# Mamba's rows of B and C put on all partitions by DMA, products with B on GpSimd, decays in PSUM

## What is computed

```python
def step(h, inp):
    d, b, c, ut = inp
    dA = jnp.exp(d[:, :, None] * A)
    h = dA * h + (d * ut)[:, :, None] * b[:, None, :]
    y = jnp.einsum('bdn,bn->bd', h, c)
    return (h, y)
...
dbc = xi @ x_proj_w.T
dt, Bm, Cm = (dbc[..., :DTR], dbc[..., DTR:DTR + N], dbc[..., DTR + N:])
delta = jax.nn.softplus(dt @ dt_proj_w.T + dt_proj_b)
A = -jnp.exp(A_log)
y = _selective_scan(xi, delta, A, Bm, Cm, D)
```

## Time and profile before

| | us |
|---|---|
| three runs | 5142.54, 5144.87, 5150.86 |
| median | 5144.87 |
| the profiled execution | 5146.39 |
| its span, first to last instruction | 5144.6 |

### The profile page before, as it was taken

One profiled execution on the slowest core, in us unless ns is written; L12 is line 12 of the kernel. 1 busy time (PEld: TensorE's weight loads), 2 busy tenths in 40 slices (PEclk: granted clock), 3 DMA queues, 4 the chain that ended last, 5 costly groups with the idle time before them and its releaser, 6 DMA issues.

```text
span 5144.6 us, 78859 instructions
## 1 busy us (share of the span) xinstructions
PE 3804.3 (74%) x26314; PEld 2426.5 (47%) x26314; DVE 3237.1 (63%) x7543; ACT 2009.1 (39%) x3158; POOL 302.5 (6%) x802
## 2 busy tenths in 40 slices
PE   2868878766877797866687788877588688786655
PEld 1645545333664464533465545543257455453333
DVE  2534983886554587388555388567755559838834
ACT  1223445343333443534333344544334344453422
POOL 0000000100000000000101000000000000000000
PEclk6979999887887998888798899988789799888867
DMA  6020011112121002020221101111211200112021
GB/s 210 1 93 3 1 42 42 52 42 99 52 83 58 1 1 67 16 93 1 99 93 46 54 1 42 42 52 42 96 52 46 93 1 1 42 42 76 17 95 44
DMA packets 162758, 261.09 MB, mean 51 GB/s; under 512 B 10960, under 2 KB 119856, under 8 KB 161968
## 3 DMA queue, kind: packets, MB, share of 16 engines
q1 hardware_dynamic: 162352, 255.91, 14.6%
HBM read 164.73 MB, written 91.15 MB: 50 GB/s over the span
## 4 chain that ended last, share of the span: by engine, by line
issue 49%; PE 27%; DVE 11%; DMA 4%; ACT 4%; POOL 3%; SPq 2%; DVEq 0%; POOLq 0%; ACTq 0%
PE bank L1641 4%; PE bank L1652 3%; PE bank L1853 3%; POOL sb_rs L1409 2%; PE bank L984 2%; PE bank L963 2%; PE bank L911 1%; DVE sb_big L2040 1%; PE bank L942 1%; PE bank L966 1%; DMA sb_big<-key_parts 1%; DVE sb_small L1227 1%; DMA key_parts<-sb_big 1%; PE bank L488 1%; PE bank L543 1%
## 5 line engine op out<-in xcount | busy, mean ns | idle before, releaser
L1112 ACT ACTIVATE sb_big<-bank 77x512 f32<-77x512 f32 (+1 forms) x512 | 303.0, 593 | 489.0 <-PE bank L984 434.4
L963 PE MATMUL bank<-sb_big 128*77 128x128 bf16 (+1 forms) x2560 | 358.7, 231 | 165.7 <-issue 74.3
L1853 PE MATMUL bank<-sb_big,sb_weights_const 128*128 128x512 f32 x768 | 472.6, 718 | 0.0
L1924 ACT ACTIVATE sb_big<-sb_big,sb_Aneg 128x512 f32<-128x512 f32 x512 | 356.6, 715 | 296.4 <-DVE sb_big L2040 267.0
L2040 DVE TENSOR_TENSOR_SCAN sb_big<-sb_big 128x512 f32<-128x512 f32 x384 | 459.0, 1210 | 0.5 <-issue 0.5
L1835 PE MATMUL bank<-sb_big,sb_sel 96*128 96x512 bf16 x512 | 216.0, 429 | 327.4 <-DVE sb_big L2047 175.2
L1227 DVE TENSOR_REDUCE sb_small<-bank 128x4 f32<-128x308 f32 (+1 forms) x512 | 265.0, 523 | 305.9 <-PE bank L942 293.4
L963 PEld LDWEIGHTS bank<-sb_big 128*77 128x77 bf16 (+1 forms) x2560 | 269.8, 115 | 258.2 <-issue 201.8
L1409 POOL TENSOR_TENSOR sb_rs<-sb_ve,sb_weights_const 128x4 f32<-128x4 f32 x112 | 120.9, 1079 | 3137.0 <-DVE sb_ve L1395 3137.0
L966 PE MATMUL bank<-sb_topT,sb_pick 128*77 128x128 bf16 (+1 forms) x2048 | 300.5, 227 | 0.0
L1652 PE MATMUL bank<-sb_weights_L1f,sb_big 128*128 128x128 f32 x2048 | 282.3, 282 | 12.3 <-DVE sb_x L1721 11.7
(11 more groups left out here) (333 smaller groups left out, 7756.7 us busy)
## 6 DMA issues: line engine op xcount, KB each, us to landing
sb_big<-query_parts SPq DMA_DIRECT2D x160, 512.0 KB, 6.4
query_parts<-sb_big SPq DMA_DIRECT2D x120, 384.0 KB, 3.3
sb_big<-key_parts SPq DMA_DIRECT2D x64, 512.0 KB, 8.9
sb_big<-context_key_parts SPq DMA_DIRECT2D x64, 308.0 KB, 4.0
key_parts<-sb_big SPq DMA_DIRECT2D x48, 384.0 KB, 4.4
context_key_parts<-sb_big SPq DMA_DIRECT2D x48, 231.0 KB, 3.9
sb_big<-masked_key_parts SPq DMA_DIRECT2D x32, 308.0 KB, 3.8
masked_key_parts<-sb_big SPq DMA_DIRECT2D x24, 231.0 KB, 3.8
```

Source lines behind the costliest of these rows:

```text
L963: last = pe.matmul(dst, A.k(s)[0:A.rows, h, ck], A.q(s)[0:A.rows, h, cq], start=True, stop=A.linear)
L1112: act.activation(A.pT(s, u).rearrange("p a b -> p (a b)"), A.psum(s, ("shifted", u))[0:A.Tk, :], ACT.Exp, scale=A.scale).then_inc(*g.one(" ...
L1853: last = pe.matmul(m.bank[s][2 + half][:, :], m.const["ident"], M.h(s, 2 * (n % 2) + half), start=n == 0, stop=n == NS - 1)
L1924: act.activation(M.dA(s, half), M.dl(s, half), ACT.Exp, scale=m.Aneg[:, NS * half + n:NS * half + n + 1])\
```

## The change

The rows of B and C are no longer spread by PE. The projection makes them once, on 32 partitions, in f32. ACT copies them to SBUF (`rows`), SP writes them to a DRAM tensor of 32 x 512 (`state_rows`), and SP reads them back with every partition reading the same row: B in pairs of rows into two buffers of 128 x 2 x 512, C row by row into two buffers of 128 x 512. SP issues a pair of B when Pool has used the pair two before, and a row of C when DVE's second product with C of two states before is done. The first read of a direction waits until the write has landed.

The products with B move to Pool, in SBUF. They wait for the row pair, for `du`, and from the third state on for PE's addition of the state two before. The decays are written to PSUM banks 0 and 1, which the spreads had. DVE's order in a state was in, in, scan, scan, out, out; now it is scan, out, scan, out. DVE's five instructions for the bf16 parts go.

```diff
-                "bc3": k_tiles(cat(bc, bc, bc)), "xdt": k_tiles(xp[:, :DTR]),
+                "bc": k_tiles(bc), "xdt": k_tiles(xp[:, :DTR]),
...
     def dA(self, s, half):
-        return cut(self.m.big[s], 5424 + 512 * half, N)
+        return self.m.bank[s][half][:, :]
+
+    def c_row(self, s, n):
+        return cut(self.m.big[s], 5168 + 512 * (n % 2), N)
...
+    def rows(self, s):
+        return self.h(s, 2)[0:2 * NS]
+
+    def b_rows(self, s, pair):
+
+        return cut(self.m.big[s], 8192 + 1024 * (pair % 2), 2, N)
...
-        yield M.at(way, 0.13)
-        spread(0, 0)
-        spread(0, 1)
         for n in range(NS):
-            if n + 1 < NS:
-                yield M.scan_at(way, n, 0.5)
-                spread(n + 1, 0)
-                yield M.scan_at(way, n, 1.1)
-                spread(n + 1, 1)
             for half in range(2):
-                yield M.scan_at(way, n, 1.1 + 0.2 * half)
+                yield M.scan_at(way, n, 0.6 + 0.5 * half)
                 pe.wait_ge(*g.at("sc_d", (way, n, "out", half)))
...
+        act.wait_ge(*g.at("mb_pe", ("bc", way)))
+        act.activation(M.rows(s), m.bank[s][0][0:2 * NS, :], ACT.Copy).then_inc(*g.one("mb_a", ("rows", way)))
         act.wait_ge(*g.at("mb_pe", ("xdt", way)))
...
+    for way in range(2):
+        for n in range(NS):
+            for half in range(2):
+                yield M.at(way, 0.115) if n == 0 else M.scan_at(way, n - 1, 0.2 + 0.4 * half)
+                if n == 0:
+                    pool.wait_ge(*g.at("mb_d", ("du", way, half)))
+                if n % 2 == 0 and half == 0:
+                    pool.wait_ge(*g.landed("rb%d" % (n // 2 % 2), (way, n // 2)))
+                if n == 0 and half == 0:
+                    pool.wait_ge(*g.at("mb_d", ("abs", way, 1)))
+                if n >= 2:
+                    pool.wait_ge(*g.at("sc_y", (way, n - 2, half)))
+                pool.tensor_tensor(M.h(s, 2 * (n % 2) + half), M.b_rows(s, n // 2)[:, n % 2, :], M.du(s, half), ALU.mult)\
+                    .then_inc(*g.one("sc_in", (way, n, half)))
+
+
+def mamba_sp(sp, g, m, M):
+    s = g.s
+    for way in range(2):
+        yield M.at(way, 0.05)
+        sp.wait_ge(*g.at("mb_a", ("rows", way)))
+        sp.dma_start(m.db[s], M.rows(s)).then_inc(*g.landing("wb", way))
+        for n in range(NS):
+            pair = n // 2
+            if n == 0:
+                yield M.at(way, 0.08)
+                sp.wait_ge(*g.landed("wb", way))
+            elif n >= 4 and n % 2 == 0:
+                yield M.scan_at(way, n - 3, 0.1)
+                sp.wait_ge(*g.at("sc_in", (way, n - 3, 1)))
+            if n % 2 == 0:
+                sp.dma_start(M.b_rows(s, pair), m.db[s][None, n:n + 2, :].to_broadcast([128, 2, N]))\
+                  .then_inc(*g.landing("rb%d" % (pair % 2), (way, pair)))
+            if n >= 2:
+                yield M.scan_at(way, n - 2, 1.1)
+                sp.wait_ge(*g.at("sc_d", (way, n - 2, "out", 1)))
+            sp.dma_start(M.c_row(s, n), m.db[s][None, NS + n, :].to_broadcast([128, N]))\
+              .then_inc(*g.landing("rc%d" % (n % 2), (way, n)))
...
         for n in range(NS):
             for half in range(2):
-                yield M.scan_at(way, n, 0.15 * half)
-                dve.wait_ge(*g.at("sc_bc", (way, n, 0)))
-                if n >= 2:
-                    dve.wait_ge(*g.at("sc_y", (way, n - 2, half)))
-                h = M.h(s, 2 * (n % 2) + half)
-                dve.tensor_tensor(h, m.bank[s][0][:, :], M.du(s, half), ALU.mult)\
-                   .then_inc(*g.one("sc_d", (way, n, "in", half)))
-            for half in range(2):
-                yield M.scan_at(way, n, 0.33 + 0.17 * half)
+                yield M.scan_at(way, n, 0.1 + 0.5 * half)
                 dve.wait_ge(*g.at("sc_da", (way, n, half)))
-                dve.wait_ge(*g.at("sc_d", (way, n, "in", half)))
+                dve.wait_ge(*g.at("sc_in", (way, n, half)))
                 h = M.h(s, 2 * (n % 2) + half)
                 dve.tensor_tensor_scan(h, M.dA(s, half), h, 0.0, ALU.mult, ALU.add)\
                    .then_inc(*g.one("sc_d", (way, n, "scan", half)))
-            for half in range(2):
-                yield M.scan_at(way, n, 0.67 + 0.16 * half)
-                dve.wait_ge(*g.at("sc_bc", (way, n, 1)))
+                yield M.scan_at(way, n, 0.35 + 0.5 * half)
+                dve.wait_ge(*g.landed("rc%d" % (n % 2), (way, n)))
                 dve.wait_ge(*g.at("sc_d", (way, n, "scan", half)))
-                h = M.h(s, 2 * (n % 2) + half)
-                dve.tensor_tensor(h, m.bank[s][1][:, :], h, ALU.mult)\
+                dve.tensor_tensor(h, M.c_row(s, n), h, ALU.mult)\
```

55 lines of the change are left out of this document (18 added, 37 removed).

## The result

| | before | after |
|---|---|---|
| median | 5144.87 us (5142.54 to 5150.86) | 5123.21 us (5111.99 to 5125.48) |
| ratio | | 0.9953, 95% interval 0.9938 to 0.9967 |
| profiled execution, span | 5146.39, 5144.6 us | 5122.35, 5120.5 us |
| 16 stretches | 1681.7 us | 1715.7 us |
| rest of the span | 3462.9 us | 3404.8 us |

The change makes the kernel faster by 22 us, 0.5%. The direction was right and the time lies in the range, but I had written 100 us. The stretches (a direction of Mamba each, from the start of its first scan to the end of its last) should have shrunk by 85 us and grew by 34. All of the gain stands outside them.

What follows compares the result with a forecast made beforehand. DVE, 92% busy, was taken to set the pace in the Mamba stretches; -310 + 40 + 75 + 10 - 15 + 50 + 10 + 40 = -100 us from 5146.4 gave 5046, so 5045 us as median, range 4920 to 5215.

Steps and rivals of the forecast that it cites:

- The spreads on PE go: PE in the Mamba stretches: PE is not late in three of four kinds, so dropping the spreads was booked at nothing.
- Other engines take over: Mamba stretches: a fifth of DVE's net 195 us shows up as waits for other chains, 40 us lost, 0 to 100.
- the port: Products with C, now reading two SBUF tensors, meet Pool 512 times: 0.15 us held per product, 75 us lost.
- the pattern rights itself: Pool and DVE in Mamba's loop: after a hold, Pool runs beside the scans again, keeping holds nearer the undisturbed row.
- rival 1: The 512 products with C: Pool's contention becomes the bound, mean hold above 0.35 us, slower at 5226 us; chance 0.20.
- the 310 us of products that leave DVE: Mamba's loop: 512 products with B move to Pool, 0.605 us of DVE's queue each, 310 us gained.
- A product with C right behind its scan: DVE's queue: overlap lost between scan and product, 0.11 us for each of 512, 56 us at most, 40 taken.
- Rows by DMA: Rows of C behind read bursts in the third and second kinds of stretch: 12.5 us a pass, 50 lost, 20 to 100.
- Decays in PSUM: ACT's decays: nothing booked for the place, 10 us lost for less cover before the next scan.
- Set-up: Start of each direction: five small DVE instructions go, 44 us in 16 directions, 15 us gained, between 0 and 44.
- What would show it: Signs in the trace after: stretches 1590 to 1605 us, DVE busy about 1305, products with C below 0.85 us mean.

Runs made afterwards that it cites:

- e10: The change but with products with B kept on DVE, and DVE's order and PE's additions as before the change: 5122.67 us, ratio 0.9968.
- e6: The changed kernel with DVE's order scan, scan, product, product and PE's additions at 1.1 and 1.3 of a state: 5028.29 us, ratio 0.9794.
- e4: The changed kernel with PE's additions planned half a state later, at 1.1 and 1.6: 5074.61 us, ratio 0.9874.
- e1: The changed kernel with Pool's 512 products cut from 512 to 32 columns each, all waits kept: 4998.02 us, ratio 0.9723.
- e8: e7 with Pool's products cut to 32 of 512 columns: 4968.16 us, ratio 0.9669.
- e3: The changed kernel with DVE's order put back to scan, scan, product, product, additions left at 0.6 and 1.1: 5304.93 us, ratio 1.0317.
- e11: The kernel before with PE's additions planned at 0.6 and 1.1, which moved the second from 1.3 to 1.1: 5204.70 us, ratio 1.0121.
- e7: The changed kernel with PE's additions half a state later and a third buffer for rows of C: 5049.48 us, ratio 0.9829.
- e2: The changed kernel with products with C reading the decay's PSUM bank instead of their row, the next decay waiting for the product: 5083.95 us, ratio 0.9887.
- e5: The changed kernel with three buffers for rows of C instead of two, rows asked for a state earlier: 5096.07 us, ratio 0.9920.
- e12: e9 with PE's additions another 0.2 of a state later, at 1.3 and 1.5: 5050.65 us, ratio 0.9813.
- e9: The changed kernel with scan, scan, product, product, additions at 1.1 and 1.3, and three buffers for rows of C: 5008.54 us, ratio 0.9743.

## Why the prediction was right or wrong

The runs split the way from before to after into four steps. The last moves PE's additions alone; the second also moves DVE's planned places a little, and the third also moves the second addition from 1.3 to 1.6.

| step | runs | us, by medians (5144.87 for before) | us, by ratios |
|---|---|---|---|
| rows by DMA, decays in PSUM, no spreads, no parts | before, e10 | -22 | -16 |
| products with B from DVE to Pool | e10, e6 | -94 | -89 |
| DVE's order scan, product | e6, e4 | +46 | +41 |
| PE's additions at 0.6 and 1.1 | e4, after | +49 | +41 |

The ratios have intervals of 5 to 15 us to either side. Each step is read at the place in the sequence where it stands; in another sequence the figures would differ, as e1 and e8 do.

**The step that failed** is "The spreads on PE go. ... They hide nothing else; booked at nothing." I looked at what PE no longer does and not at where the rest of it now stands. The diff moves the first addition half a state and the second a fifth of a state forward. So PE's head of queue is an addition whose product DVE has not made, and the other stream's work stands behind it. e4 prices it at 49 us in the change (63 us of DVE's idle time in the stretches), e3 at 277 us where the products are later as well. e11 shows, with a smaller move, that the place of the additions costs time by itself. "Other engines take over", a fifth of DVE's gain or 40 us, was meant for waits of this kind but took PE's busy share as its measure. PE at 68% busy does not say that an addition is on time. That the idle time still came to 115 us against 110 booked is luck. Rows took 49, Pool's products and norms 10, decays nothing, and all other chains 57 against 40 booked. e4, with PE's additions later, has 63 us less idle time, so their place accounts for all of the 57.

**The second step that failed** is the size of the port, 75 us on the products with C and nothing on DVE's other instructions. By the table of DVE's time this is where the sum missed most: products with C, scans and all others took some 210 us more, and 115 were booked for the port and the order together. A clock as the cause is not borne out: the granted clock of the run was 0.864 before, 0.855 in the change and 0.850 in e4, the faster of the two. How much of the small gain of e10 (0.851) it ate, no run separates.

**The port**: mechanism and place right, size too small. I had booked 0.15 us per product, 75 us; measured is 0.21 us (884 - 675 ns), 105 us in duration. The prediction's own figure for a Pool that starts at random, half of the starts at 0.4 us, is 0.20; what failed is the belief that the pattern rights itself. What I left out entirely is that DVE's other instructions are held too: some 45 us in duration. On the path both together are worth 81 us (e8 against e7) to 125 us (e1 against after). The line at which rival 1 was to decide, a mean hold of 0.35 us, was not reached. Taken the other way, e6 against e10: of the 310 us of products that leave DVE, 94 us reach the end. In the stretches 293 us of products with B go; the products with C take back 88 us, the scans 4, DVE's other instructions 45 (12 more of them fall inside), and idle time 70, which leaves 85 us. The Trainium skill (SBUF — State Buffer, Who interferes with whom) names the pair that contends, two SBUF inputs on DVE against Pool; e1 and e2 agree, 688 and 686 ns once Pool's side is short or DVE's has a bank.

**A product with C right behind its scan**: 40 us booked, 46 measured as the whole effect of the order. The size fits; the reason is broader than the one given, so that is in part luck. Counted in the trace of after, 240 of the 512 products directly follow their scan, 34 ns behind its end, where before they overlapped by some 79 ns: about 27 us. From e6 to e4 the stretches grow by 69 us. The scans take 21 us more, which is the lost overlap; the products with C take 21 us more (172 held in place of 115) and the others 36 us (20 more of them fall inside), while idle time falls by 9 us. The rest of the span shrinks by 15 us.

**Rows by DMA**: the place and its length were right. The timelines of DVE and SP's queue in the third kind of stretch, to be read against the earlier trace rows:

```profile
953.88 0.74 DVE L2053 TENSOR_TENSOR sb_big<-sb_big 128x512 f32<-128x512 f32 x1 [2.14 <-DMA sb_big<-state_rows]
...
967.49 0.69 DVE L2053 TENSOR_TENSOR sb_big<-sb_big 128x512 f32<-128x512 f32 x1 [9.87 <-DMA sb_big<-state_rows]
```
```profile
956.52 0.55 SPq L1350 DMA_DIRECT2D sb_big<-key_parts  x1
957.12 0.54 SPq L1978 DMA_DIRECT2D sb_big<-state_rows  x1
```

The row goes out directly behind the eighth read and is waited for 9.87 us; 10 were foreseen. In all 48.7 us of idle time before the larger group, against 50 booked; all but 0.3 us of it is in the third kind, 12 us a pass, and the second kind, with 10 booked, has next to none. e5, which removes 33 of the 49 us, gains 27 us (17 by the ratios) and moves other things too. So the term was right as idle time, and what the stall costs at the end is not settled. Undisturbed rows landed as foreseen, in 3.4 us (median of 256), pairs of B in 4.4 (page after):

```profile
sb_big<-state_rows SPq DMA_DIRECT2D x128, 512.0 KB, 4.4
sb_big<-state_rows SPq DMA_DIRECT2D x256, 256.0 KB, 3.4
```

**Decays in PSUM**: 10 us booked for less cover, none seen; in the change no scan waited for ACT, the idle before the larger group was 7.3 us, by Pool. The place in PSUM is free, as booked: scans 1213 ns against 1210.

**Set-up**: 15 us booked, not shown. In e10 the time outside the stretches is 14.8 us shorter than before, but in e11, whose set-up is that of the kernel before, it is 13.8 us shorter too (5201.1 - 1752.2 = 3448.9). Between the two directions of a block, where the dt chain lies, the eight gaps sum to 303 us before and 301 in e10, so the chain did not shorten, as foreseen. In the change itself the rest of the span shrank by 58 us: 18 of it in these gaps. The 32 products with B that lay outside the stretches, some 19 us, are part of the 58; the rest has no owner that a run shows. Longer stretches do not explain it: e3 has the longest stretches (1850) and 3447 us outside, e1 short ones (1603) and 3388.

**What would show it**: median product with C 0.68 to 0.69 us (held), mean below 0.85 (0.884, not held), Pool's products between 1.27 and 1.9 us (median 1.28, five longer than 1.9, up to 2.66), scans at 1.21 (held), about 10 us of idle in the third kind (held), stretches at 1590 to 1605 (1716, not held). The stretches at 1587 are what e6 shows, with PE's and DVE's places of before.

**Left open**: what makes Pool fall into a scan more often in e12 than in e9; why more of the freed time turns idle in e8 than in e1; and what shortened the time outside the stretches.

## What to carry to other kernels

Where streams share in-order queues, a change is priced twice: by the instructions that it adds and removes, and by the place of every waiting instruction that it re-plans; the planned place of PE's additions alone cost 49 us here (41 by the ratios), so undo each one by itself before judging the idea, and look in the queue for what the line of the plan really moved. Work moved from DVE to Pool leaves DVE only in part: time comes back on DVE's products of two SBUF tensors, and on the other stream's norms too. And a result near zero may hide a good change under a bad one: with PE's and DVE's planned places put back and one more row buffer, the same change gains 2.6% instead of 0.5%.

## What had not been expected of the hardware

- Pool's products also hold small instructions: a norm's 128x128 subtraction and scaling, with one tensor and two columns as inputs, took 1.28 us at 699.23 and 398 ns in the mean against 342, and 343 once the Pool products were short (e1). I had thought only of instructions with two tensors of 128x512. Not every instruction on SBUF is held: the 64 norm statistics in the stretches, which read one 128x128 tensor, took 277 ns in the mean, before and after.
- With Pool at 1.28 us in the median and a scan at 1.21 us, the order of the queues alone changed how often Pool's product met a product with C: the number of 512 that were held by more than 0.1 us was 79 in e3 and 188 after, which differ in DVE's order, and 112 in e9 and 165 in e12, which differ in PE's additions.
- A read that puts one DRAM row of 512 or two on all 128 partitions landed in 3.4 and 4.4 us, not later than a plain 512 KB read of the query stacks (6.6 us, page after). All three are medians, with what stood in the queue.
